# A four-layer graph kernel on one core: the last phase in another order, minus mean over deviation on GpSimd, and longer load rings

## The reference

```
L0: agg = eps*x + adj@x;  h = silu(rmsnorm(agg@W1 + b1));  h@W2 + b2
L1: GRU(concat(conv(x), exp(-dist(x))*mask @ relu(x@w_msg + b)), x)
L2: ht = h@W.T;  curr = adj_norm@curr three times;  leaky_relu(sum conv_w[k]*curr + conv_b)
L3: agg = (1+eps)*x + adj@x;  relu(agg@W1 + b1)@W2 + b2
layernorm(y) = (y - mean) / sqrt(var + eps)
```

## Time and profile before

| | |
|---|---|
| median of 3 runs | 1172.59 us (1169.11 to 1173.3) |
| the profiled execution | 1173.6 us, of which 1171.8 us is its span |
| mean granted TensorE clock | 0.985 of full speed |
| busy share | PE 94%, DVE 71%, ACT 59%, POOL 48% |
| phase three | from 485.14 us to 1171.8 us |

### The profile page before, as it was taken

One profiled execution on the slowest core, in us unless ns is written; L12 is line 12 of the kernel. 1 busy time (PEld: TensorE's weight loads), 2 busy tenths in 40 slices (PEclk: granted clock), 3 DMA queues, 4 the chain that ended last, 5 costly groups with the idle time before them and its releaser, 6 DMA issues.

```text
span 1171.8 us, 25210 instructions
## 1 busy us (share of the span) xinstructions
PE 1102.7 (94%) x8267; PEld 990.0 (84%) x8267; DVE 833.5 (71%) x2596; ACT 694.8 (59%) x1296; POOL 563.0 (48%) x524
## 2 busy tenths in 40 slices
PE   7899999999999789899999999999999999999874
PEld 6799999999999679788888888888888888888774
DVE  4477778787777533146887778877787878877974
ACT  4444555555555332256677777767776776767665
POOL 1244433434342235335555555656555565656654
PEclk9999999999999899899999999999999999999998
DMA  4122332223232255411111121211212121220000
GB/s 156 55 64 75 99 91 91 91 91 91 91 91 64 73 168 180 155 50 58 34 40 54 47 65 47 65 38 47 65 47 65 47 65 40 64 65 10 20 28 36
DMA packets 47110, 82.62 MB, mean 71 GB/s; under 512 B 5316, under 2 KB 15368, under 8 KB 46728
## 3 DMA queue, kind: packets, MB, share of 16 engines
q1 hardware_dynamic: 46984, 81.02, 22.5%
HBM read 55.31 MB, written 25.69 MB: 69 GB/s over the span
## 4 chain that ended last, share of the span: by engine, by line
PE 81%; DVE 9%; issue 6%; ACT 2%; DMA 1%; SPq 0%; POOL 0%; DVEq 0%; POOLq 0%; ACTq 0%
PE banks L156 16%; PE banks L465 9%; PE banks L150 9%; PE banks L151 8%; PE banks L152 8%; PE banks L722 4%; PE banks L631 3%; PE banks L632 3%; PE banks L493 3%; PE banks L558 2%; PE banks L609 2%; PE banks L435 2%; DVE stats L1019 2%; DVE prop L1214 2%; PE banks L587 2%
## 5 line engine op out<-in xcount | busy, mean ns | idle before, releaser
L163 POOL TENSOR_TENSOR rstd<-ve,minus_half 128x4 f32<-128x4 f32 x128 | 130.5, 1020 | 101.9 <-DVE ve L1029 98.8
L163 POOL TENSOR_TENSOR r_rms<-ms,minus_half 128x4 f32<-128x4 f32 x32 | 32.3, 1008 | 224.2 <-DVE ms L993 224.2
L465 PE MATMUL banks<-w,s 128*128 128x128 f32 x768 | 101.2, 275 | 0.4 <-DVE y L1007 0.4
L465 PEld LDWEIGHTS banks<-w,s 128*128 128x128 f32 x768 | 95.6, 192 | 3.4 <-issue 0.5
L150 PE MATMUL banks<-agg_hi,w_hi 128*128 128x512 f32 x192 | 82.4, 429 | 10.1 <-issue 8.6
L1373 POOL TENSOR_TENSOR y<-leaky,x_rows 128x512 f32<-128x512 f32 x32 | 42.6, 1331 | 97.3 <-ACT x_rows L922 96.8
L1019 DVE BATCH_NORM_STATS2 stats<-y 128x6 f32<-128x128 f32 x384 | 82.9, 278 | 1.7 <-POOL y L1373 1.6
L1359 POOL TENSOR_TENSOR x3b<-x_rows,late_rows 128x512 f32<-128x512 f32 x32 | 40.9, 1278 | 82.5 <-DVE y L1239 82.5
L160 ACT ACTIVATE agg_hi<-banks 128x512 fp32r<-128x512 f32 x64 | 38.2, 597 | 64.7 <-PE banks L156 36.1
L151 PE MATMUL banks<-agg_lo,w_hi 128*128 128x512 f32 x192 | 76.4, 398 | 0.0
L152 PE MATMUL banks<-agg_hi,w_lo 128*128 128x512 f32 x192 | 76.3, 398 | 0.0
(11 more groups left out here) (192 smaller groups left out, 3401.1 us busy)
## 6 DMA issues: line engine op xcount, KB each, us to landing
at<-in_at SPq DMA_DIRECT2D x32, 256.0 KB, 2.9
x_rows<-in_x SPq DMA_DIRECT2D x32, 256.0 KB, 2.9
x_scratch<-x SPq DMA_DIRECT2D x32, 256.0 KB, 3.2
ad<-in_ad SPq DMA_DIRECT2D x32, 256.0 KB, 2.7
x1c<-x_scratch SPq DMA_DIRECT2D x32, 256.0 KB, 2.7
atc<-in_at SPq DMA_DIRECT2D x32, 256.0 KB, 2.9
yh<-yh_scratch SPq DMA_DIRECT2D x32, 256.0 KB
out<-out_rows SPq DMA_DIRECT2D x32, 256.0 KB, 3.1
```

What stands on the lines that cost most here:

```text
L163: return nc.gpsimd.tensor_tensor(to[:], base[:], minus_half[:], ALU.pow)
L465: last = pe.matmul(bank[7][:, g, :], s[c][:, g, :], w2[:, c, :], start=(c == 0 and g == 0), stop=(c == H0 - 1), skip_group_check=True)
```

## The change

1. `minus_mean` moves from VectorE (one instruction per norm) to GpSimd (two: times minus one, then times the mean, with a wait between them), right behind `norm` of layers 2 and 3.
2. All four engines get another list of stages. The gates' products with the messages and the convolution, `gate_z`, `gate_u` and so on are done one turn later (t - 2 in place of t - 1), as are the hops, `y1_t` and layer 3's `hidden3`. The number of turns stays 41.
3. Steps get other PSUM banks. `messages` and `y1_t` now share bank 7, `tz` is read from bank 1, `gate_n` and `gather` share bank 4, `hidden_n`, `hop2` and `hop3` bank 3, `inverse`, `gather3` and the second `hidden3` bank 6. The `free` lists follow.
4. `X1C_RING, ATC_RING` are 6 and 11 in place of 4 and 8. SyncE's own code is unchanged.

```diff
-        X1C_RING, ATC_RING, YH_RING, OUT_RING = 4, 8, 2, 2
+        X1C_RING, ATC_RING, YH_RING, OUT_RING = 6, 11, 2, 2
...
             def distances(k):
                 until(pe, "pts_l", k)
                 until(pe, "pts_r", k)
-                free(pe, ("prop", k - 5), ("v", k - 2), ("edge", k - 1))
-                free(pe, ("factor_r pts_r", k), ("t2", k - 5), ("edge", k - 1))
-                free(pe, ("agg3_hi agg3_lo", k - 7), ("msg", k), ("z1", k - 8), ("edge", k - 1))
-                free(pe, ("xn_hi xn_lo", k - 1), ("z0", k - 8), ("edge", k - 1))
+                free(pe, ("factor_r pts_r", k), ("y3", k - 9), ("edge", k - 1))
+                free(pe, ("tz", k - 2), ("edge", k - 1))
+                free(pe, ("t2", k - 5), ("ht", k - 5), ("edge", k - 1))
+                free(pe, ("ghn", k - 1), ("prop", k - 6), ("t1", k - 6), ("edge", k - 1))
...
             def y1_t(k):
                 until(pe, "y1", k)
-                free(pe, ("x2_rows", k - 1))
+                free(pe, ("msg", k + 4), ("x2_rows", k - 1))
...
-            def minus_mean(k, n):
-                until(dve, ("r2", "r3")[n], k)
-                until(dve, ("x3_rows", "out_rows")[n], k - 1)
-                V.scalar_tensor_tensor(out=nm[n][:], in0=mv[2 + n][:, :, 0], scalar=-1.0, in1=rstd[2 + n][:],
-                                       op0=ALU.mult, op1=ALU.mult).then_inc(sem[("nm2", "nm3")[n]], 1)
...
+            def minus_mean(k, n):
+                until(pool, ("r2", "r3")[n], k)
+                Q.tensor_scalar(minus_rstd[n][:], rstd[2 + n][:], -1.0, None, ALU.mult
+                                ).then_inc(sem[("minus_r2", "minus_r3")[n]], 1)
+                until(pool, ("minus_r2", "minus_r3")[n], k)
+                Q.tensor_tensor(nm[n][:], minus_rstd[n][:], mv[2 + n][:, :, 0], ALU.mult
+                                ).then_inc(sem[("nm2", "nm3")[n]], 1)
...
-                stage(gate_nmp, t - 1, R_GATE)
-                stage(distances, t)
+                stage(inverse, t)
+                stage(distances, t)
```

More of the change, by code:

```diff
@@ L605, in messages @@
                 landed(pe, x1c_in, k)
-                free(pe, ("z1", k - 8), ("edge", k - 1), ("agg3_hi agg3_lo", k - 8), ("msg", k - 1))
-                pe.matmul(flat(bank[2]), pick[:], flat(msg_bias), start=True, stop=False, skip_group_check=True)
+                free(pe, ("x2_rows", k - 5), ("msg", k - 1))
+                pe.matmul(flat(bank[7]), pick[:], flat(msg_bias), start=True, stop=False, skip_group_check=True)
                 for g in range(G):
-                    last = pe.matmul(bank[2][:, g, :], x1c[k % X1C_RING][:, g, :], msg_w[:], start=False,
+                    last = pe.matmul(bank[7][:, g, :], x1c[k % X1C_RING][:, g, :], msg_w[:], start=False,
                                      stop=(g == G - 1), skip_group_check=True)
@@ L628, in inverse @@
                 landed(pe, yh_in, k, 32)
-                free(pe, ("ghn", k - 1), ("y3", k - 8), ("c2_res", k - 1))
+                free(pe, ("agg3_hi agg3_lo", k - 8), ("z1", k - 9), ("c2_res", k - 1))
                 for g in range(G):
@@ L655, in gate_nmp @@
                 if gate == N_GATE:
[L656 removed]
+                    free(pe, ("xn_hi xn_lo", k), ("v", k - 1))
                 last = split_product(pe, flat(bank[GATE_BANK[gate]]), *weight(IH + 2 * gate + 1), flat(xn_hi),
@@ L688, in hop2 @@
                 until(pe, "t2", k)
-                free(pe, ("tr", k + 3), ("t1", k - 1))
-                by_graph(pe, bank[4], lambda g: atc[k % ATC_RING][:, g, :], lambda g: t2[:, g, :]
+                free(pe, ("edge", k + 5), ("ghn", k + 4), ("prop", k - 1), ("t1", k - 1))
+                by_graph(pe, bank[3], lambda g: atc[k % ATC_RING][:, g, :], lambda g: t2[:, g, :]
                          ).then_inc(sem["hop2_ps"], 1)
@@ L694, in hop3 @@
                 until(pe, "t1", k)
-                free(pe, ("v", k + 3), ("edge", k + 4), ("prop", k - 1))
-                by_graph(pe, bank[0], lambda g: atc[k % ATC_RING][:, g, :], lambda g: t1[:, g, :]
+                free(pe, ("t1", k), ("edge", k + 5), ("ghn", k + 4), ("prop", k - 1))
+                by_graph(pe, bank[3], lambda g: atc[k % ATC_RING][:, g, :], lambda g: t1[:, g, :]
                          ).then_inc(sem["hop3_ps"], 1)
@@ L719, in down3 @@
                 if c == 0:
-                    free(pe, ("c2_res", k + 7), ("ghn", k + 6), ("y3", k - 1))
+                    free(pe, ("edge", k + 8), ("factor_r pts_r", k + 8), ("y3", k - 1))
                 for g in range(G):
-                    last = pe.matmul(bank[6][:, g, :], z3[c][:, g, :], w32[:, c, :], start=(c == 0 and g == 0),
+                    last = pe.matmul(bank[0][:, g, :], z3[c][:, g, :], w32[:, c, :], start=(c == 0 and g == 0),
                                      stop=(c == H3 - 1), skip_group_check=True)
```

201 lines of the change are left out of this document (100 added, 101 removed).

## The result

The changed kernel takes 1165.18 us in the median (1159.41 to 1169.22, 20 runs), against 1172.94 (1166.45 to 1177.77, 20 runs) for the kernel before. The ratio is 0.994, with a 95% interval from 0.9926 to 0.9954. The forecast was 1160 (1150 to 1173), faster. Direction and range were right, and of the forecast gain of 12.6 us 7.8 came.

| part | before | after | difference | forecast |
|---|---|---|---|---|
| up to the first `codes` of phase three | 485.1 | 486.6 | +1.4 | 0 |
| fill, turns 0 to 8 | 129.4 | 124.7 | -4.7 | -6.5 |
| middle, turns 9 to 31 | 469.2 | 453.4 | -15.8 | -10.8 |
| drain, turns 32 to 40 | 88.0 | 99.1 | +11.1 | +5.0 |

What follows compares the result with a forecast made beforehand. TensorE was taken as the bound (busy 94%, 81% of the chain). Fill -6.5, middle -10.8 and drain +5.0 gave -12.3 us on the span, 1171.8 to 1159.5; on the runs' scale 1160 us, range 1150 to 1173.

Steps and rivals of the forecast that it cites:

- The wait that goes: TensorE's wait for `agg3_lo` ahead of `distances`, 0.66 us a turn, was to go whatever `nm` costs.
- the middle: Turns 9 to 31: 23 turns of 19.85 us against 20.23, half the slow-clock loss counted, minus 10.8 us.
- the new wait of 0.28 ahead of `y1_t`: Bank 7, `msg` to `y1_t`: TensorE ready at 13.46 but free to start at 13.74, 0.28 us each turn.
- it just holds: Bank 1, `tz` to `distances`: TensorE could start at 9.33 us of the turn and is there at 9.43.
- The two turns with a low clock: Two longer turns in 9 to 31, 3.7 us in all; half was counted as gained.
- The fill: Turns 0 to 8: 8.7 us of work put off, turn 0 some 1.5 longer, minus 6.5 us in sum.
- The drain: Turns 32 to 40: put-off work returns, a loop through all engines sets turns 34 and 35; 93 against 88, plus 5.0.
- a sign of being wrong: The prediction called itself wrong if a turn took 20.2 or more, TensorE waited at `distances`, or turns 32 to 40 exceeded 98.
- Minus mean on GpSimd: Four small GpSimd instructions a turn, 0.8 us each, 1.7 a pair with the wait; no cost in turns 9 to 31.
- The rings: SyncE's buffers: with `ya` one turn later four would be short, six enough; nothing gained or lost, 0.
- The rivals: Wait only moves, 1169 us (0.17); ScalarE's queue sets the turn, 1185 (0.13); clock, 1196 (0.04); under 1151 (0.06).
- the clock rival: Short waits at a new place lower TensorE's clock each turn, 1.7 us a turn, 1196 us in all; chance 0.04.

Runs made afterwards that it cites:

- the kernel with the old rings: The changed kernel with X1C_RING and ATC_RING back at 4 and 8, SyncE's order unchanged: 1321.9 us, ratio 1.1254 against the kernel before.

## Why the prediction was right, and where a size was off

**The wait that goes, and the middle.** Right in its mechanism: the wait ahead of `distances`, worth 0.66 a turn, is gone, and `nm` has no part in that in the new order, as `minus_mean` back on VectorE shows. The turn was forecast at 19.85 and is 19.70. The term that was off is the new wait of 0.28 ahead of `y1_t`: it is 0.05. I had given PE 0.36 us from the end of its releaser to its start, read at a release by VectorE. At `tz` that fits (it ends at 758.19, L600 begins at 758.54), and would be the 0.12 there, where I wrote "it just holds". At `msg` it doesn't: that ends at 762.60, and L672 begins at 762.74. Why the two differ stays open. 23 turns of 0.15 less are 3.5 us. The two turns with a low clock didn't come back, and I had counted half of what they cost. (My 3.7 for them is 3.9 by the rows: 469.2 less 23 times 20.23.) Together 5.4, against the 5.0 by which the middle came out shorter than forecast.

**The fill.** The work put off was right. Turn 0 was taken at +1.5 and is +3.5. I had priced `distances` and `messages` behind `inverse` at full clock, at 0.43 and 1.12. Behind the 5.17 us in which PE stands they took 3.18 together (496.10 to 499.28). `inverse` itself is no part of this: its steps are 0.43 long in place of 0.22 in turn 0 of both kernels. Turns 0 and 1 together are still 0.7 shorter than before. `inverse` behind `messages` gives 2.7 back.

**The drain.** This is the mis-sized term, +11.1 for +5.0. At 99.1 it is over the 98 that I had named as a sign of being wrong, so of the drain the forecast was wrong. In turn 34 I put `prop` at 3.3 and `y1_t` at 8.5 from the turn's start at 1093.64. VectorE's timeline after:

```profile
1094.29 1.45 DVE L1186 SCALAR_TENSOR_TENSOR yb<-tz,nn 128x512 f32<-128x512 f32 x1
...
1096.45 1.10 DVE L1214 SCALAR_TENSOR_TENSOR prop<-banks,row_inv,w0h 128x128 f32<-128x128 f32 x4
...
1101.64 1.34 DVE L1197 TENSOR_SCALAR x_rows<-banks,mv,rstd 128x128 f32<-128x128 f32 x4
```

`prop` ends at 3.9, `x2_rows` at 9.3, and `y1_t` begins at 9.5: 1.0 late. What stands behind `y1_t` was taken at 4.7 and took 6.4 (1103.13 to 1109.54), with a clock of 0.79 in that turn: `y1_t` took 1.08 in place of 0.44, and each step of the split product 0.43 in place of 0.23. In turn 35 the loop was even 0.6 shorter than laid out (7.9), but what stands behind took 6.1. With the clock held up there it took 4.7 (1116.65 to 1121.39), as laid out. At the end I laid out a round from one `gather3` to the next as 5.4. The chain after has it at 7.9:

```profile
1141.26 0.91 PE banks L156 x8
...
1144.81 0.43 PE banks L151
...
1146.94 2.19 PE banks L722 x16
1149.13 0.91 PE banks L156 x8
```

The split products go in steps of 0.43 in place of 0.23, which makes 1.2 for the six, and the two `down3` took 2.19 in place of 1.78. The rest are round trips that I had set too short. The other 1.1 of turns 37 and 38 lies in turn 37. The chain of before had a whole round to read, at 7.3, with its split products at the low clock as well:

```profile
1152.78 0.53 PE banks L150
...
1160.12 0.47 PE banks L150
```

So these lengths came from the middle, where PE is hardly ever idle and its clock is full, and were set down in a drain where neither holds.

**Minus mean on GpSimd.** "Costs nothing in the middle" was right, the price was not. I took 0.8 an instruction, nearest to the power's 1.02, with 0.53 as the lower bound. They took 0.23 and 0.20, under the bound: both rows that I had bounded it by are of 128 columns or more, and these have four. And I didn't ask what the move alone would do where `nm` still stood ahead of `agg_lo`: it takes the whole wait there, at once. I had written only that in the new order the wait goes whatever `nm` costs.

**The rings.** "A ring of four would be short" was right in its sign. I saw it as a load that lands late for itself, and in my expectation of the run I even took it back. What counts is the queue: the load of `yh` behind it.

**The rivals.** None came. PE starts 0.12 late at `distances`, where it waited 0.56, and 0.05 late at `y1_t`, and the clock is 1.00 over the whole middle. What the clock rival feared did come in the kernel with the old rings, behind waits of some 3 us in each turn: its clock is 0.87. (The time that I gave for this rival, 1196, is 1199 by my own numbers: 1172.6 and 39 less 12.3.)

**Luck.** The span is 4.3 us over its forecast. That is 1.4 from phases one and two, 1.8 from the fill and 6.1 from the drain, less 5.0 in the middle. That the total came out so near is in part luck, since the two largest misses cancel.

## What to carry to other kernels

Try each part of a change alone: here one of its parts, moved by itself, took 22 us off (1172.7 to 1150.4), and with the new order around it 8. The new order was laid out for the repeating turn, and its drain is 13.8 us longer. Price a drain from rows of a drain, with their clock and their round trips, not from the full turn's lengths. When a buffer ring is short, look at who is queued behind the waiting load, because that is what the engine missed here. And count a wait of TensorE together with the clock behind it.

## What the runs showed of the hardware that I had not expected

- A small instruction on GpSimd is cheap, and the power is not: on the same 128x4 tile a one-input product took 0.23 us, a two-input product 0.20, and the power 1.02.
- A four-column instruction on VectorE with two inputs in SBUF took 0.15 us at one place of the turn and 1.20 at another. In the earlier trace rows the long one ends 0.02 behind a full tile of GpSimd. The Trainium skill, "GPSIMD Engine Reference", section "Key points", calls VectorE about twice as fast at elementwise work. With GpSimd idle the trace agrees in direction, with 0.15 against 0.20 and 0.23. Where the two meet the measurement says otherwise: 0.5 for the pair on GpSimd, 1.2 on VectorE.
- One load that waits in SyncE's queue cost 157 us over the whole kernel (1164.95 with `yh` ahead of it, 1321.9 with `yh` behind it, the rings being the same). By the estimate above more than half of that is the low clock behind the waits, and not the waits.
- Matmuls added in the gaps of a drain brought the clock from 0.88 to 1.00 in one turn, and from 0.79 to 0.89 in another, where the time didn't fall. In the old order they brought the whole drain from 0.92 to 1.00, and it took 82.85 in place of 85.34.
